# Far scores of a causal attention: two row tiles of 128 columns, or one block-diagonal product of 256

## The chip, the cores and the metric

The kernel runs on one core of one Trainium2 chip. The time is the device time of one execution in microseconds (us), the median over several runs. Before the change it is 4056.7 us over three runs (4050.87 to 4056.8). The profile is of one further execution, which took 4048.82 us, 4047.1 us of them between its first and its last instruction.

## The reference

The block has four batches of 2048 tokens, width 256, 16 heads of 16 dimensions.

```python
q, k, v = split_heads(x @ Wq + bq), split_heads(x @ Wk + bk), split_heads(x @ Wv + bv)
scores = jnp.einsum('bhid,bhjd->bhij', q, k)
rel = jnp.einsum('bhid,pd->bhip', q, rel_key)          # p = 512 relative positions
rel_idx = jnp.clip(j - i + p - 1, 0, p - 1)            # all keys 511 or more back share position 0
bias = jnp.take_along_axis(rel, rel_idx, axis=3)
logits = jnp.where(j <= i, (scores + bias) * scale, -inf)
out = jnp.einsum('bhij,bhjd->bhid', softmax(logits), v) @ Wo + bo
```

The reference calls it as `x + ga * attn(modulated layernorm(x))`, followed by a mixture of eight experts of which each token uses two. Only the attention is touched here.

## The kernel before, in words

The kernel has four phases one after the other: modulation, projection, attention and experts. In the attention, queries and keys are cut into blocks of 128 tokens, 16 blocks a batch. For each row of blocks i the kernel scores key blocks j = 0 to i. A block is **near** if i - j < 5: then each product also needs a bias that depends on the distance. It is **far** otherwise: then all keys share the bias of relative position 0, which is already folded into the keys, and a far score is a plain product.

Queries and keys are float16 pairs of a high and a low part, so that one head's product has a contraction of 3 x 16 rows and one more row that subtracts the row maximum, 49 in all (`KM` = 48). Two heads lie in one tile of 128 partitions: heads 0 to 7 in partitions 0 to 48, heads 8 to 15 in partitions 64 to 112. The keys of both are in `kn[:, j, h]`. The queries are in `qs[:, slot, e, h]`, block-diagonal: `qs` is cleared once and for e = 0 only partitions 0 to 63 are filled, for e = 1 only 64 to 127. A near product (`near_scores`, L775) uses all 113 rows and gets both heads from one weight load, with 32 queries of each. A far product (`far_scores`, L789) names 49 rows of one half, and 128 queries.

Each row of blocks is visited twice. First come its **maxima**, two rows ahead of the scores (`AHEAD` = 2): PE makes the products again in one of three PSUM banks `pm` (`NBUF` = 3), and DVE takes each bank of 512 columns into `acc` by an elementwise maximum (L721 the first, L725 near, L733 far). Then come 16 transposes (`turn`, L816), a reduction over the keys (L736), one more transpose (`rows`, L820), and the maxima go through memory into row 48 of `qs`. The **scores** themselves go to two PSUM tiles `ps` of two banks each. ACT takes the exponential of a tile in one instruction (L758 near, L761 far), and `weigh` (L845) multiplies the values, 32 columns of the array at a time.

The order is written out in `batch`. For each pair (i, j) there are three places: score half 0, score half 1, and weigh the pair before. The list of steps of `max_steps(i + 2)` is spread evenly over the places by its number of entries: a near block gives four steps of one bank, a far block two steps of two banks. Every engine walks the same order. PE may start a maximum only when DVE has emptied the bank it writes to (`mx_done`). Because a far step fills two banks, it waits for the bank two tiles back, `done_count(b, n + 1 - NBUF)`; a near step waits for the one three tiles back.

Of the kernel before, what the change touches and what calls it, by code (L numbers as in the profile page):

```python
# [26 lines left out]
ALU = mybir.AluOpType  # L27
ACT = mybir.ActivationFunctionType
# [7 lines left out]
P = 128  # L36
NB = S // P
EH = E // P
HH = 8
# [4 lines left out]
SCALE = D ** -0.5  # L44
# [420 lines left out]
def phase_attention(nc, io, keep):  # L465
# [4 lines left out]
    AHEAD, SLOTS, NBUF = 2, 4, 3  # L470
    KM = 3 * D
# [12 lines left out]

    def max_steps(i):

        out = []
        for j in key_order(i):
            out += [("near", j, x) for x in range(4)] if near(home(i), j) else [("far", j, r) for r in range(2)]
        return out + [("turn", 0, r) for r in range(4)] + [("rows", 0, 0)]  # L490

    def after_same(i, j):

        js = key_order(i)
        return near(home(i), js[js.index(j) - 1]) == near(home(i), j)

    in_bank = lambda step: 2 if step[0] == "far" else 1
    max_tiles = lambda i: sum(map(in_bank, max_steps(i)))
    first_tile = lambda i: sum(max_tiles(n) for n in range(i))
    NT = first_tile(NB)  # L500
    assert NT % NBUF == 0 and NP % 4 == 0

    def batch_maxima(maximum, b, i, steps, start, stop):
        n = first_tile(i) + sum(map(in_bank, steps[:start]))
        for step in steps[start:stop]:
            maximum(b, i, *step, n)
            n += in_bank(step)

    def batch(b, last, score=None, weigh=None, maximum=None, step=None):

# [32 lines left out]
    with PhaseMemory(nc, "att") as a:  # L543
# [36 lines left out]
        with nc.Block() as block:  # L580
# [126 lines left out]
            @block.vector  # L707
            def _(dve):
                dve.memset(qs[:, :, :, :, :], 0.0).then_inc(cleared, 1)
                dve.memset(tick[:, 0:1], 0.0).then_inc(pair_done[0], HALF)  # L710
                dve.memset(tick[:, 1:2], 0.0).then_inc(pair_done[1], HALF)
                dve.memset(tick[:, 2:3], 0.0).then_inc(mx_done, NBUF)

                def maximum(b, i, kind, j, r, n):
                    u = i % 2
                    if kind == "near":
                        dve.wait_ge(mx_full, b * NT + n + 1)
                        held = acc[:, u, :, r * XQ:(r + 1) * XQ]
                        got = pm[n % NBUF][:, :].rearrange("p (h c) -> p h c", c=XQ)
                        if j == home(i):  # L720
                            dve.tensor_copy(held, got).then_inc(mx_done, 1)  # L721
                        else:

                            dve.wait_ge(mx_done, done_count(b, n - 4 if after_same(i, j) else n - r - 1))
                            dve.tensor_tensor(held, got, held, ALU.max).then_inc(mx_done, 1)  # L725
                    if kind == "far":
                        for e in range(2):
                            dve.wait_ge(mx_full, b * NT + n + e + 1)
                            held = acc[:, u, e * HH + 4 * r:e * HH + 4 * r + 4, :]
                            got = pm[(n + e) % NBUF][:, :].rearrange("p (h c) -> p h c", c=P)  # L730

                            dve.wait_ge(mx_done, done_count(b, n + e - 4 if after_same(i, j) else n - 2 * r - 1))
                            dve.tensor_tensor(held, got, held, ALU.max).then_inc(mx_done, 1)  # L733
                    if kind == "turn":
                        dve.wait_ge(mx_full, b * NT + n + 1)
                        dve.reduce_max(mx[:, u, 4 * r:4 * r + 4], pm[n % NBUF][:, :].rearrange("p (h k) -> p h k", k=P),  # L736
                                       AX.X).then_inc(mx_done, 1)
                    if kind == "rows":
                        dve.wait_ge(mx_full, b * NT + n + 1)
                        dve.wait_ge(m_in[u], b * (NB // 2 * 32) + i // 2 * 32)  # L740
                        dve.tensor_copy(mrow[:, u, :], pm[n % NBUF][0:H, 0:P]).then_inc(mx_done, 1)  # L741

                def weigh(b, i, j, k):
                    if j < i:
                        return
                    dve.wait_ge(pair_done[k % 2], pair_count(b, k))
                    dve.wait_ge(on_out[i % 2], b * (NB // 2 * 16) + i // 2 * 16)
                    dve.tensor_copy(on[:, i % 2], po[:, :, :]).then_inc(on_done, 1)
                order(dve, maximum=maximum, weigh=weigh)

            @block.scalar
            def _(act):
                def score(b, i, j, k, t):
                    act.wait_ge(s_full[t], b * NP + k + 1)

                    act.wait_ge(pair_done[k % 2], pair_count(b, k) - 1)
                    if near(i, j):
                        act.activation(pt[:, k % 2, :, t * 64:t * 64 + 64].rearrange("p h (x c) -> p x h c", x=2),  # L758
                                       ps[t][:, :, :].rearrange("p x (h c) -> p x h c", c=XQ), ACT.Exp, scale=SCALE).then_inc(p_done[t], 1)
                    else:  # L760
                        act.activation(pt[:, k % 2].rearrange("p (e h) c -> p e h c", e=2)[:, :, 4 * t:4 * t + 4, :],  # L761
                                       ps[t][:, :, :].rearrange("p e (h c) -> p e h c", c=P), ACT.Exp, scale=SCALE).then_inc(p_done[t], 1)
                order(act, score=score)

            @block.tensor
            def _(pe):
# [16 lines left out]
                                             start=False, stop=(g == XQ // G - 1), skip_group_check=True)  # L783
                    return last

                def far_scores(bank, i, j, e, h, c):

                    s, rows = i % SLOTS, slice(64 * e, 64 * e + KM + 1)
                    return pe.matmul(bank[:, c * P:(c + 1) * P], kn[rows, j, h, :], qs[rows, s, e, h, :],  # L789
                                     start=True, stop=True, skip_group_check=True)  # L790

                def maximum(b, i, kind, j, r, n):
                    if kind == "near" and j == home(i) and r == 0:
                        pe.wait_ge(qs_in[i % SLOTS], b * (NB // SLOTS * 64) + i // SLOTS * 64 + 64)
                        pe.wait_ge(spread, b * NB + i + 1)
                    if kind == "near":
                        keys = kn[:, j] if i < NB else kx[:, j]
                        if r == 0 and (j == home(i) or i == AHEAD):
                            if i < NB:
                                pe.wait_ge(kv_in[j], b * 80 + 80)  # L800
                            else:
                                pe.wait_ge(kx_in, b * (AHEAD * 64) + AHEAD * 64)
                        pe.wait_ge(mx_done, done_count(b, n - NBUF))
                        near_scores(pm[n % NBUF][:, :], keys, i, j, r, False).then_inc(mx_full, 1)
                    if kind == "far":
                        pe.wait_ge(mx_done, done_count(b, n + 1 - NBUF))
                        pe.wait_ge(built, 80)
                        for c in range(4):
                            for e in range(2):
                                last = far_scores(pm[(n + e) % NBUF][:, :], i, j, e, 4 * r + c, c)  # L810
                                if c == 3:
                                    last.then_inc(mx_full, 1)
                    if kind == "turn":
                        pe.wait_ge(mx_done, done_count(b, max(n - NBUF, n - 1 - r)))
                        for h in range(4):
                            last = pe.transpose(pm[n % NBUF][:, h * P:(h + 1) * P], acc[:, i % 2, 4 * r + h, :], keep["ident"][:, :])  # L816
                        last.then_inc(mx_full, 1)
                    if kind == "rows":
                        pe.wait_ge(mx_done, done_count(b, n - 1))
                        pe.transpose(pm[n % NBUF][0:H, 0:P], mx[:, i % 2, :], keep["ident"][:, :]).then_inc(mx_full, 1)  # L820

                def score(b, i, j, k, t):
# [5 lines left out]
                    if near(i, j):  # L828
                        for x in range(2):
                            last = near_scores(ps[t][:, x], kn[:, j], i, j, 2 * t + x, True)  # L830
                        last.then_inc(s_full[t], 1)
                    else:
                        pe.wait_ge(built, 80)
                        for c in range(4):
                            for e in range(2):
                                last = far_scores(ps[t][:, e], i, j, e, 4 * t + c, c)
                        last.then_inc(s_full[t], 1)

                def weigh(b, i, j, k):
# [704 lines left out]
```

## Time and profile before

| | |
|---|---|
| median of three runs | 4056.7 us |
| profiled execution | 4048.82 us, span 4047.1 us |
| PE busy (matmul) | 3370.2 us, 83% |
| PE weight loads | 2904.3 us, 72% |
| DVE busy | 2355.8 us, 58% |
| ACT busy | 1486.2 us, 37% |
| attention (303.5 to 3053 us) | 2749.5 us |

PE is the matmul engine, DVE the vector engine, ACT the scalar engine and POOL the general one. Matmuls are pipelined: a row "0.40 us, x8" in a timeline is eight matmuls, each of which is shown for some 0.2 us, with much of that lying over its neighbours. So what a group costs PE is the distance from its start to the start of the next group. Ends of matmuls are modelled, and starts are recorded.

### The profile page before, as it was taken

The page shows a single profiled execution, that of the slowest core. Times are in us where ns is not written, and L with a number is a line of the kernel's source. Part 1 is how long each engine was busy: PE and PEld are TensorE (multiplying, and loading weights), DVE is VectorE, ACT ScalarE, POOL GpSimd, SP SyncE. Part 2 cuts the span into 40 slices and gives each one's busy share as a digit, 9 for nine tenths or more (in the row PEclk, how much of TensorE's full clock was granted, in tenths as well). Part 3 has the DMA queues.
Part 4 walks back from the last instruction along what each step waited for, and adds up shares of the span by engine and source line. Part 5 has one row for each costly group of instructions (what it writes and reads, how often), then busy time and mean ns, then how long its engine had stood idle before and what let it go on. Part 6 is the DMA issues. An engine that isn't in the chain of part 4 may idle for free. (4 is left out here: it accounts for less than half of the span.)

```text
span 4047.1 us, 177336 instructions
## 1 busy us (share of the span) xinstructions
PE 3370.2 (83%) x76680; PEld 2904.3 (72%) x76680; DVE 2355.8 (58%) x4401; ACT 1486.2 (37%) x1799; POOL 1093.1 (27%) x936
## 2 busy tenths in 40 slices
PE   6956999999899999999999999999995877599910
PEld 4535887778888777888877788887774766488800
DVE  5844666773566677166667536666722666466633
ACT  1311233446233344623334542334461322255511
POOL 1013311111322111232211133111101555422266
PEclk8977999999999999999999999999996766599955
DMA  4763100001210000310100031000006976333356
GB/s 121 210 154 99 38 24 27 23 23 56 84 31 30 23 23 13 99 46 28 29 21 24 23 106 43 23 23 23 11 9 102 171 141 125 107 116 116 113 166 179
DMA packets 275046, 285.87 MB, mean 71 GB/s; under 512 B 99208, under 2 KB 212716, under 8 KB 274156
## 3 DMA queue, kind: packets, MB, share of 16 engines
q1 hardware_dynamic: 248044, 214.34, 20.5%
q0 software_dynamic: 26240, 60.20, 5.4%
q8 instruction: 621, 10.17, 1.0%
q14 instruction: 141, 1.16, 0.1%
HBM read 165.64 MB, written 107.53 MB: 67 GB/s over the span
## 5 line engine op out<-in xcount | busy, mean ns | idle before, releaser
L758 ACT ACTIVATE att_pt<-att_ps 128x1024 f32<-128x1024 f32 x560 | 574.1, 1025 | 1206.2 <-PE att_ps L782 1206.2
L725 DVE TENSOR_TENSOR att_acc<-att_pm,att_acc 128x512 f32<-128x512 f32 x864 | 570.7, 688 | 351.0 <-PE att_pm L779 343.6
L733 DVE TENSOR_TENSOR att_acc<-att_pm,att_acc 128x512 f32<-128x512 f32 x1056 | 666.3, 685 | 146.2 <-PE att_pm L789 137.7
L779 PE MATMUL att_ps<-att_qx,table_x 68*128 68x64 f16 x8960 | 720.5, 194 | 0.3 <-issue 0.2
L782 PE MATMUL att_ps<-att_qz,table_z 128*128 128x64 f16 x8960 | 717.7, 193 | 0.4 <-issue 0.4
L761 ACT ACTIVATE att_pt<-att_ps 128x1024 f32<-128x1024 f32 x528 | 515.1, 1024 | 381.8 <-PE att_ps L789 380.5
L782 PEld LDWEIGHTS att_ps<-att_qz,table_z 128*128 128x128 f16 x8960 | 613.3, 98 | 0.4 <-issue 0.3
L779 PEld LDWEIGHTS att_ps<-att_qx,table_x 68*128 68x128 f16 x8960 | 610.6, 98 | 1.0 <-issue 1.0
L845 PE MATMUL att_po<-att_pt,att_vn 128*32 128x128 f32 x17408 | 590.1, 276 | 0.5 <-issue 0.3
L683 POOL DMA_DIRECT2D s_m<-att_mrow x64 | 35.3, 552 | 1817.5 <-DVE att_mrow L741 1790.7
L775 PE MATMUL att_pm<-att_qs,att_kn 113*128 113x64 f16 x8672 | 444.7, 195 | 52.0 <-POOL att_qx L668 45.0
L775 PE MATMUL att_ps<-att_qs,att_kn 113*128 113x64 f16 x8960 | 449.1, 193 | 38.7 <-DMA att_qs<-s_m 32.5
L845 PEld LDWEIGHTS att_po<-att_pt,att_vn 128*32 128x32 f32 x17408 | 443.4, 110 | 48.0 <-issue 11.0
L779 PE MATMUL att_pm<-att_qx,table_x 68*128 68x64 f16 x8960 | 455.0, 194 | 1.8 <-issue 1.7
L775 PEld LDWEIGHTS att_pm<-att_qs,att_kn 113*128 113x128 f16 x8672 | 328.8, 99 | 132.3 <-issue 57.1
L775 PEld LDWEIGHTS att_ps<-att_qs,att_kn 113*128 113x128 f16 x8960 | 344.1, 98 | 66.8 <-issue 46.6
L779 PEld LDWEIGHTS att_pm<-att_qx,table_x 68*128 68x128 f16 x8960 | 347.9, 99 | 2.6 <-issue 2.5
L736 DVE TENSOR_REDUCE att_mx<-att_pm 128x4 f32<-128x512 f32 x256 | 172.1, 690 | 282.1 <-PE att_pm L816 282.1
L721 DVE COPY att_acc<-att_pm 128x512 f32<-128x512 f32 x256 | 172.1, 688 | 216.1 <-PE att_pm L779 215.1
L789 PE MATMUL att_pm<-att_qs,att_kn 49*128 49x128 f16 x4224 | 209.5, 219 | 92.5 <-DVE att_acc L733 91.8
L668 POOL TENSOR_TENSOR att_qz<-att_qe,mask_i 128x1024 f16<-128x1024 f16 x128 | 240.4, 1901 | 57.4 <-DMA att_qe<-s_q 56.2
L668 POOL TENSOR_TENSOR att_qx<-att_qe,mask_i 64x1024 f16<-64x1024 f16 x128 | 239.2, 1887 | 0.0
(214 smaller groups left out, 4172.2 us busy)
## 6 DMA issues: line engine op xcount, KB each, us to landing
att_qe<-s_q SPq DMA_DIRECT2D x256, 128.0 KB
moe_xs<-s_h SPq DMA_DIRECT2D x71, 256.0 KB, 2.7
s_y<-moe_y SPq DMA_DIRECT2D x71, 256.0 KB, 2.1
s_v<-prj_vx SPq DMA_DIRECT2D x32, 512.0 KB, 3.7
att_vn<-s_v SPq DMA_DIRECT2D x64, 256.0 KB, 3.4
s_o<-att_on POOLq DMA_DIRECT2D x64, 256.0 KB, 3.2
att_qs<-s_q SPq DMA_DIRECT2D x128, 66.0 KB
prj_x<-in_x POOLq DMA_DIRECT2D x16, 512.0 KB, 4.6
```

Source lines behind the costliest of these rows:

```text
L668: last = pool.tensor_tensor(dst[0:rows, s, :, heads, :], qe[0:rows, i % 2, heads].rearrange("p h (g i) -> p g h i", i=G), keep["mask_i"][0 ...
L721: dve.tensor_copy(held, got).then_inc(mx_done, 1)
L725: dve.tensor_tensor(held, got, held, ALU.max).then_inc(mx_done, 1)
L733: dve.tensor_tensor(held, got, held, ALU.max).then_inc(mx_done, 1)
L736: dve.reduce_max(mx[:, u, 4 * r:4 * r + 4], pm[n % NBUF][:, :].rearrange("p (h k) -> p h k", k=P), AX.X).then_inc(mx_done, 1)
L758: act.activation(pt[:, k % 2, :, t * 64:t * 64 + 64].rearrange("p h (x c) -> p x h c", x=2), ps[t][:, :, :].rearrange("p x (h c) -> p x h ...
L761: act.activation(pt[:, k % 2].rearrange("p (e h) c -> p e h c", e=2)[:, :, 4 * t:4 * t + 4, :], ps[t][:, :, :].rearrange("p e (h c) -> p e ...
L775: pe.matmul(pairs[:, :, h], keys[0:rows, h, :], qs[0:rows, s, :, h, x * XQ:(x + 1) * XQ], start=(h == 0), stop=False, skip_group_check=True)
L779: last = pe.matmul(groups[:, :, g], keep["table_x"][:, y:y + P], qx[0:G * D + G, s, x * (XQ // G) + g], start=False, stop=(g == XQ // G - ...
L782: last = pe.matmul(groups[:, :, g], keep["table_z"][:, y:y + P], qz[:, s, x * (XQ // G) + g], start=False, stop=(g == XQ // G - 1), skip_g ...
L789: return pe.matmul(bank[:, c * P:(c + 1) * P], kn[rows, j, h, :], qs[rows, s, e, h, :], start=True, stop=True, skip_group_check=True)
L845: last = pe.matmul(po[32 * (h % 4):32 * (h % 4) + 32, h // 4, :], vn[:, j, h, :], pt[:, k % 2, h, :], start=(j == 0 and h < 4), stop=(j == ...
```

## The change

A far product now names all 113 rows, as the near one does, and takes the queries of both heads from the block-diagonal `qs`: 2 x 128 = 256 columns from one weight load. One bank of 512 columns is filled by two such products and holds heads h and h + 8 side by side. So a far block of maxima becomes four steps of one bank, in place of two steps of two banks, and waits for the bank three tiles back. The number of banks filled (`NT`), the number of DVE and ACT instructions and their sizes are as they were; their views of `acc` and `pt` follow the new order of heads. Because a far block now has four entries in the list, the even spreading over the places puts the steps of a row elsewhere.

```diff
-            out += [("near", j, x) for x in range(4)] if near(home(i), j) else [("far", j, r) for r in range(2)]
+        out = [("near" if near(home(i), j) else "far", j, x) for j in key_order(i) for x in range(4)]
...
-                    if kind == "far":
-                        for e in range(2):
-                            dve.wait_ge(mx_full, b * NT + n + e + 1)
-                            held = acc[:, u, e * HH + 4 * r:e * HH + 4 * r + 4, :]
-                            got = pm[(n + e) % NBUF][:, :].rearrange("p (h c) -> p h c", c=P)
+                            held = acc[:, u].rearrange("p (e h) c -> p h e c", e=2)[:, 2 * r:2 * r + 2]
+                            got = pm[n % NBUF][:, :].rearrange("p (h e c) -> p h e c", e=2, c=P)
...
-                def far_scores(bank, i, j, e, h, c):
-                    s, rows = i % SLOTS, slice(64 * e, 64 * e + KM + 1)
-                    return pe.matmul(bank[:, c * P:(c + 1) * P], kn[rows, j, h, :], qs[rows, s, e, h, :],
-                                     start=True, stop=True, skip_group_check=True)
+                def far_scores(bank, i, j, r):
+                    s, rows = i % SLOTS, 64 + KM + 1
+                    for h in range(2):
+                        last = pe.matmul(bank[:, 2 * h * P:(2 * h + 2) * P].rearrange("p (e c) -> p e c", c=P), kn[0:rows, j, 2 * r + h, :],
+                                         qs[0:rows, s, :, 2 * r + h, :], start=True, stop=True, skip_group_check=True)
+                    return last
...
                     if kind == "far":
-                        pe.wait_ge(mx_done, done_count(b, n + 1 - NBUF))
-                        pe.wait_ge(built, 80)
-                        for c in range(4):
-                            for e in range(2):
-                                last = far_scores(pm[(n + e) % NBUF][:, :], i, j, e, 4 * r + c, c)
-                                if c == 3:
-                                    last.then_inc(mx_full, 1)
+                        pe.wait_ge(mx_done, done_count(b, n - NBUF))
+                        far_scores(pm[n % NBUF][:, :], i, j, r).then_inc(mx_full, 1)
...
-                        for c in range(4):
-                            for e in range(2):
-                                last = far_scores(ps[t][:, e], i, j, e, 4 * t + c, c)
+                        for x in range(2):
+                            last = far_scores(ps[t][:, x], i, j, 2 * t + x)
```

PE in row 13 of a batch, among its far pairs, before the change. Writes to `att_ps` are scores, to `att_pm` maxima of row 15, to `att_po` the weighing; L775 with L779 is one near maximum.

```order
L845 MATMUL att_po<-att_pt,att_vn 32x128 x16
L806 REGISTER_ALU
L789 MATMUL att_pm<-att_qs,att_kn 128x128 x8
L827 REGISTER_ALU
L789 MATMUL att_ps<-att_qs,att_kn 128x128 x8
L806 REGISTER_ALU
L789 MATMUL att_pm<-att_qs,att_kn 128x128 x8
L789 MATMUL att_ps<-att_qs,att_kn 128x128 x8
L803 REGISTER_ALU
L775 MATMUL att_pm<-att_qs,att_kn 128x2x32 x8
L779 MATMUL att_pm<-att_qx,table_x 128x16x4 x8
L845 MATMUL att_po<-att_pt,att_vn 32x128 x16
```

Here a far maximum fills two banks with eight products, and one stands behind each weighing or score. After the change, in the same row (L766 and L770 are the near maximum, L781 is `far_scores`, L831 the weighing):

```order
L815 REGISTER_ALU
L781 MATMUL att_ps<-att_qs,att_kn 128x256 x4
L799 REGISTER_ALU
L781 MATMUL att_pm<-att_qs,att_kn 128x256 x2
L799 REGISTER_ALU
L781 MATMUL att_pm<-att_qs,att_kn 128x256 x2
L781 MATMUL att_ps<-att_qs,att_kn 128x256 x4
L799 REGISTER_ALU
L781 MATMUL att_pm<-att_qs,att_kn 128x256 x2
L799 REGISTER_ALU
L781 MATMUL att_pm<-att_qs,att_kn 128x256 x2
L831 MATMUL att_po<-att_pt,att_vn 32x128 x16
```

The four banks of a far block now come one by one, two behind each score half, each with a wait of its own.

## Rows read from the trace of the kernel before

**Rows 1.** The page: busy time of each engine, and PE's clock in 40 slices.

```profile
PE 3370.2 (83%) x76680; PEld 2904.3 (72%) x76680; DVE 2355.8 (58%) x4401; ACT 1486.2 (37%) x1799; POOL 1093.1 (27%) x936
PEclk8977999999999999999999999999996766599955
```

**Rows 2.** Windows: length, then busy PE, PEld, DVE, ACT, POOL; clock; DMA.

```profile
303.50:3053.00 2749.50, 2521.25 (x71696) 2222.08 (x71697) 1637.47 (x2559) 1092.47 (x1091) 617.08 (x507) 0.98 0.12 37
1389.50:1443.40 53.90, 49.28 (x1402) 42.55 (x1401) 37.29 (x59) 22.11 (x22) 9.78 (x8) 1.00 0.08 23
1558.60:1618.80 60.20, 55.44 (x1558) 46.82 (x1556) 43.71 (x69) 27.19 (x28) 9.79 (x8) 1.00 0.07 20
3700.00:3712.00 12.00, 11.95 (x107) 10.16 (x105) 8.08 (x15) 7.02 (x13) 3.49 (x3) 1.00 0.39 117
```

**Rows 3.** Groups of instructions on PE, the far products; count, busy, mean ns, idle before.

```profile
L789 PE MATMUL att_pm<-att_qs,att_kn 49*128 49x128 f16 x4224 | 209.5, 219 | 92.5 <-DVE att_acc L733 91.8
L789 PE MATMUL att_ps<-att_qs,att_kn 49*128 49x128 f16 x4224 | 204.6, 218 | 7.6 <-ACT att_pt L761 5.5 <-issue 0.3
```

**Rows 4.** Timeline of PE, row 12 of the second batch: start, length, engine, line.

```profile
1504.23 0.41 PE L775 MATMUL att_pm<-att_qs,att_kn 113*128 113x64 f16 x8
1504.47 0.40 PE L779 MATMUL att_pm<-att_qx,table_x 68*128 68x64 f16 x8
1504.81 0.40 PE L789 MATMUL att_ps<-att_qs,att_kn 49*128 49x128 f16 x8
1505.13 0.41 PE L775 MATMUL att_pm<-att_qs,att_kn 113*128 113x64 f16 x8
1505.38 0.40 PE L779 MATMUL att_pm<-att_qx,table_x 68*128 68x64 f16 x8
1505.71 1.08 PE L845 MATMUL att_po<-att_pt,att_vn 128*32 128x128 f32 x32
1506.72 0.41 PE L775 MATMUL att_pm<-att_qs,att_kn 113*128 113x64 f16 x8
...
1507.30 0.40 PE L789 MATMUL att_ps<-att_qs,att_kn 49*128 49x128 f16 x8
1507.53 0.39 PE L789 MATMUL att_pm<-att_qs,att_kn 49*128 49x128 f16 x8
1507.75 0.39 PE L789 MATMUL att_ps<-att_qs,att_kn 49*128 49x128 f16 x8
1508.87 0.40 PE L789 MATMUL att_pm<-att_qs,att_kn 49*128 49x128 f16 x8 [0.73 <-DVE att_acc L733]
```

**Rows 5.** Timeline of PE in the experts: twelve float16 products of 256 columns.

```profile
3703.16 1.47 PE L1440 MATMUL moe_bank<-moe_h_s,moe_w_s 128*128 128x256 f16 x12
3704.47 1.47 PE L1468 MATMUL moe_bank<-moe_w_s,moe_h_s 128*128 x12
```

**Rows 6.** Waits of PE's matmuls and weight loads: total us, times, longest.

```profile
PE att_pm L789 <- DVE att_acc L733: 91.8, 128, 1.2
PEld att_pm L789 <- DVE att_acc L733: 130.5, 200, 1.3
PEld att_ps L789 <- ACT att_pt L761: 17.7, 57, 0.7
```

**Rows 7.** Groups of instructions on DVE and ACT.

```profile
L733 DVE TENSOR_TENSOR att_acc<-att_pm,att_acc 128x512 f32<-128x512 f32 x1056 | 666.3, 685 | 146.2 <-PE att_pm L789 137.7
L725 DVE TENSOR_TENSOR att_acc<-att_pm,att_acc 128x512 f32<-128x512 f32 x864 | 570.7, 688 | 351.0 <-PE att_pm L779 343.6
L761 ACT ACTIVATE att_pt<-att_ps 128x1024 f32<-128x1024 f32 x528 | 515.1, 1024 | 381.8 <-PE att_ps L789 380.5
```

**Rows 8.** Timeline, fourth batch, row 14: far scores without maxima between.

```profile
2985.16 1.08 PE L845 MATMUL att_po<-att_pt,att_vn 128*32 128x128 f32 x32
2986.18 0.40 PE L789 MATMUL att_ps<-att_qs,att_kn 49*128 49x128 f16 x8
2986.77 0.40 PE L789 MATMUL att_ps<-att_qs,att_kn 49*128 49x128 f16 x8 [0.20 <-ACT att_pt L761]
```

More of the change, by code:

```diff
@@ L485, in max_steps @@
     def max_steps(i):
-        out = []
-        for j in key_order(i):
-            out += [("near", j, x) for x in range(4)] if near(home(i), j) else [("far", j, r) for r in range(2)]
+        out = [("near" if near(home(i), j) else "far", j, x) for j in key_order(i) for x in range(4)]
         return out + [("turn", 0, r) for r in range(4)] + [("rows", 0, 0)]
@@ L495, in after_same @@
         return near(home(i), js[js.index(j) - 1]) == near(home(i), j)
-    in_bank = lambda step: 2 if step[0] == "far" else 1
-    max_tiles = lambda i: sum(map(in_bank, max_steps(i)))
+    max_tiles = lambda i: len(max_steps(i))
     first_tile = lambda i: sum(max_tiles(n) for n in range(i))
@@ L503, in batch_maxima @@
     def batch_maxima(maximum, b, i, steps, start, stop):
-        n = first_tile(i) + sum(map(in_bank, steps[:start]))
-        for step in steps[start:stop]:
+        for n, step in enumerate(steps[start:stop], first_tile(i) + start):
             maximum(b, i, *step, n)
-            n += in_bank(step)
     def batch(b, last, score=None, weigh=None, maximum=None, step=None):
@@ L715, in maximum @@
                     u = i % 2
-                    if kind == "near":
+                    if kind in ("near", "far"):
                         dve.wait_ge(mx_full, b * NT + n + 1)
-                        held = acc[:, u, :, r * XQ:(r + 1) * XQ]
-                        got = pm[n % NBUF][:, :].rearrange("p (h c) -> p h c", c=XQ)
+                        if kind == "near":
+                            held = acc[:, u, :, r * XQ:(r + 1) * XQ]
+                            got = pm[n % NBUF][:, :].rearrange("p (h c) -> p h c", c=XQ)
+                        else:
+                            held = acc[:, u].rearrange("p (e h) c -> p h e c", e=2)[:, 2 * r:2 * r + 2]
+                            got = pm[n % NBUF][:, :].rearrange("p (h e c) -> p h e c", e=2, c=P)
                         if j == home(i):
@@ L724, in maximum @@
                             dve.wait_ge(mx_done, done_count(b, n - 4 if after_same(i, j) else n - r - 1))
-                            dve.tensor_tensor(held, got, held, ALU.max).then_inc(mx_done, 1)
-                    if kind == "far":
-                        for e in range(2):
-                            dve.wait_ge(mx_full, b * NT + n + e + 1)
-                            held = acc[:, u, e * HH + 4 * r:e * HH + 4 * r + 4, :]
-                            got = pm[(n + e) % NBUF][:, :].rearrange("p (h c) -> p h c", c=P)
-                            dve.wait_ge(mx_done, done_count(b, n + e - 4 if after_same(i, j) else n - 2 * r - 1))
                             dve.tensor_tensor(held, got, held, ALU.max).then_inc(mx_done, 1)
@@ L760, in score @@
                     else:
-                        act.activation(pt[:, k % 2].rearrange("p (e h) c -> p e h c", e=2)[:, :, 4 * t:4 * t + 4, :],
-                                       ps[t][:, :, :].rearrange("p e (h c) -> p e h c", c=P), ACT.Exp, scale=SCALE).then_inc(p_done[t], 1)
+                        act.activation(pt[:, k % 2].rearrange("p (e h) c -> p h e c", e=2)[:, 4 * t:4 * t + 4],
+                                       ps[t][:, :, :].rearrange("p x (h e c) -> p (x h) e c", e=2, c=P), ACT.Exp, scale=SCALE).then_inc(p_done[t], 1)
                 order(act, score=score)
@@ L832, in score @@
                     else:
-                        pe.wait_ge(built, 80)
-                        for c in range(4):
-                            for e in range(2):
-                                last = far_scores(ps[t][:, e], i, j, e, 4 * t + c, c)
+                        for x in range(2):
+                            last = far_scores(ps[t][:, x], i, j, 2 * t + x)
                         last.then_inc(s_full[t], 1)
```

## The prediction

> **What bounds the kernel now.** I began with the busy shares [rows 1]: PE leads with 83%, DVE has 58%, ACT 37%. The windows come next, since the change lies in the attention alone. There PE's matmuls fill 2521 of 2749.5 us and DVE is busy for 1637 [rows 2]. In the long rows of blocks it is tighter: row 13 of the second batch lasts 60.2 us, with 55.4 on PE and 43.7 on DVE; row 10 lasts 53.9, with 49.3 and 37.3 [rows 2]. So PE sets the pace and DVE is its nearest rival. The clock is at its upper level, 2.4 GHz, there (1.00). The reader should see two things in PE's rows that a busy share hides: what a far group costs from start to start, and how long PE stands before it.
>
> **The far product in PE's own time.** There are 2 x 4224 far matmuls [rows 3], that is 1056 groups of eight. Where far groups follow one another they start at 1507.30, 1507.53 and 1507.75: 0.23 us for eight products of 128 columns [rows 4]. 1024 columns at 2.4 GHz would be 0.43 us, so the two halves of the array do work side by side. The change gives this up: the same group is four products of 256 columns. The nearest rows are the experts' float16 products of 256 columns, twelve from 3703.16 to 3704.47 at clock 1.00 [rows 2, 5]: 1.31 / 12 = 0.109 us each, 0.436 a group. This adds 0.436 - 0.234 = 0.202 us, times 1056: **+213 us**. (0.234 is the 0.23 of the row, to a digit more than it prints, taken over all such neighbours of the trace.) No row shows this product with two stretches of 128 columns as its moving side. Bounds: 256 columns at 2.4 GHz are 0.107 us, 10 us less in total; the near product with its two stretches of 32 columns takes (1504.47 - 1504.23) / 8 = 0.030 us for 64 columns [rows 4], 0.120 for 256, which would be 46 us more. I take 0.109, the row with the same column count.
>
> **The borders of the far groups.** From L775 to L779 it is 0.24 us, both over the full array. From L779 to a far group it is 0.34 (1504.47 to 1504.81) and from a far group to L775 0.32 (1504.81 to 1505.13), against 0.24 and 0.23 where the kind stays [rows 4]. Each border between a far group and a full-array group so costs 0.096 us, at entry and at exit alike. Counted in the program's order there are 738 unbroken stretches of far groups; 1056 of their ends lie at full-array work and 420 at the weighing L845. The first kind goes: 1056 x 0.096 = **-101 us**. The second stays, as L779 to L845 also takes 0.33 (1505.38 to 1505.71), and L845 to L775 1.01 (1505.71 to 1506.72), where L845 to a far group takes 1.02 (2985.16 to 2986.18) [rows 4, 8]. If the border is not a matter of the row tiles, nothing of the 101 comes back.
>
> The Trainium skill, "TensorEngine Tiling (Array Packing)", has both sides of this. Its section "When to Use Tiling" wants row tiles where the contraction is 64 or less and promises up to twice the speed, which by itself speaks against this change; 49 rows fall under it, and the trace agrees with 0.23 us against 0.43. Its section "Key Properties" says that a change of tiling mode drains the engine, and the borders of 0.096 us agree with that. By the first alone the sum would be 213 us worse before any wait is counted, by both it is 112.
>
> PE's own work therefore grows by 213 - 101 = **112 us**. Fewer weight loads (one for two heads) bring nothing beyond this, since they lie under the products.
>
> **The waits that it can fill.** PE stands before far groups for DVE: 130.5 us by the weight loads, in 200 waits, and for ACT 17.7 us in 57 [rows 6]. By the matmuls it is 91.8 us [rows 6], but their ends are modelled and swallow up to 0.2 us of each wait, so I go by the loads, whose total is 148; some of them hold the ordinary pause behind a weighing, and I take **145** as what can come back. Bounds: 97 (91.8 + 5.5 of [rows 3, 6]) and 148.
>
> Why should it come back? A wait arises because a far step needs two of three banks at once and hands DVE two tiles: DVE needs about 0.63 us for a tile where it runs through (the rows say 685 ns with overlap, 666.3 us for 1056 [rows 7]). At 1508.87 PE stood 0.73 us for this [rows 4]. After the change each tile asks for one bank, the one three tiles back, and DVE's total is untouched. I walk through the piece shown in the order after the change, PE's start at 0 with a near maximum: it ends at 0.48; score half 0.92; first far tile 1.13; second 1.35; score half 1.79; third 2.01; fourth 2.23; weighing to 3.35. DVE, some 0.2 us behind and one tile each 0.63: near tile done 1.33, far tiles 1.97, 2.60, 3.23, 3.87. The third tile starts at 1.79 and needs the near tile's bank (1.33); the fourth starts at 2.01 and needs the first far one's (1.97); the next near tile starts at 3.35 and needs the second's (2.60). Nothing is waited for if DVE starts level, and some 0.1 us if it is a little behind. There are 264 far blocks of maxima, so I leave 20 us of waits between 0 (all gone) and 145 (all kept). The wait for ACT: with no maxima between, a pair of blocks is two exponentials of 0.98 us (515.1 / 528), 1.95 us, while PE has 0.23 + 0.33 + 1.01 = 1.57 us and stands for ACT: its two halves start 0.59 apart, at 2986.18 and 2986.77, in place of 0.23 [rows 7, 8]. After, PE has 0.44 + 0.56 + 1.01 = 2.01, just above. So in those pairs the longer products are mostly under ACT's time already.
>
> The steps of a row move too. In row 13, 44 tiles instead of 40 are now made under its nine far pairs. PE has about 33 us there and DVE 44 x 0.63 = 28, so PE still leads. DVE's and ACT's instructions keep count and size; the new views cost between 681 and 688 ns as all maxima of 512 columns do, under 7 us either way, on an engine with room. SP, POOL and their DMA do not move. The four transposes at the end of a row come in a little denser, with a wait of up to 0.5 us in some of 44 rows, which I cost at 5 us within the 20.
>
> **Sum.** +213 - 101 - 145 + 20 = **-13 us**. Against the profiled execution: 4048.8 - 13 = 4036. That execution lies 8 us below the median of the runs, so against the median it is 4056.7 - 13 = **4043.7 us**. A difference of 0.2% (8 us) is about what a measurement of this kernel tells from none.
>
> **Rivals.**
> - *DVE sets the pace in the far stretches* (slower). The waits stay because they are DVE's work and not its bursts: in row 13 DVE is 73% busy over the whole row, more within a burst of four far tiles, 4 x 0.63 = 2.5 us, for which PE of its own has 4 x 0.109 x 2 + 2 x 0.436 = 1.7 us. If half of the 145 stay the sum is 213 - 101 - 72 = +40, 4097 us; if all stay, +112, 4169 us. It decides as soon as more than 41 us of waits are left. For it: all far waits today name DVE. Against: with a weighing of 1.01 us behind every burst DVE catches up.
> - *No change to be measured.* The gain and the loss are each near 110 us, and 25 to 40 us of remaining waits cancel them: 4049 to 4065 us.
> - *The border cost stays*, as something other than row tiles, for example the change of operands. Then +213 - 145 + 20 = +88, 4145 us. Against: L775 to L779 changes operands as well and shows none [rows 4].
> - *All waits go and the product takes 0.107 us*: 213 - 10 - 101 - 145 = -43, 4014 us.
>
> **How the numbers follow.** My forecast, with the last rival as its lower end, has 0.54 (faster by over 0.2%); no change to be measured 0.22; slower 0.24, of which DVE's pace holds 0.19 and the borders 0.05. The time is the forecast's, 4044. The range begins at 4012, just below the all-gone case of 4014, and goes up to 4080, some 55 us of remaining waits; above lie half of the slower cases. The forecast's own range is 4014 to 4048.
>
> **What would show it.** In the changed profile far groups of four should start 0.44 us apart, the step from L779's line to a far product should be near 0.24 us, and the waits of PE's loads for the far maxima should fall from 130.5 to below 30 us. DVE's busy time should stay within 10 us of 2355.8, and PE's far busy time should rise. I am wrong if the waits stay, if the pitch of the 256-column product is not 0.109, or if waits appear before near maxima or transposes instead.

## The result

Over 20 runs each the changed kernel takes 4043.74 us (4034.22 to 4050.64) and the kernel before 4055.65 us (4038.06 to 4064.22). The ratio is 0.9972, with a 95% interval of 0.9964 to 0.9980: a gain of 0.28%, 11.9 us between the medians. The profiled execution of the changed kernel happens to be its slowest run (4050.64 us, span 4049.0), so spans say little here. What is steady is the attention's own length, and the last start of the weighing marks its end. This is that line for the kernel before and for the changed one (instruction and count; shortest, median and longest ns; first and last start in us):

```profile
L845 PE MATMUL att_po<-att_pt,att_vn x17408: 269/273/422, 378.8 to 3054.5; 128*32 128x128 f32 x198
```

```profile
L831 PE MATMUL att_po<-att_pt,att_vn x17408: 269/273/297, 380.2 to 3046.4; 128*32 128x128 f32 x198
```

The attention ends 8.1 us earlier. I use this mark for all kernels below, and call it the end mark. The first start of the weighing moves between runs too, from 378.8 to 386.3 us, so every difference at the end mark is uncertain by some 5 us, and smaller ones are not read.

### The profile page after: what moved, and what is told of

Its sections match the earlier page's. It is cut to its first block and busy times, and to the rows that moved or that the text cites. A ratio compares the mean times of both kernels' runs of the same rounds, so it can differ in the third digit from the quotient of the medians.

```text
span 4049.0 us, 168239 instructions
## 1 busy us (share of the span) xinstructions
PE 3466.8 (86%) x72456; PEld 3019.6 (75%) x72456; DVE 2363.6 (58%) x4401; ACT 1489.8 (37%) x1799; POOL 1094.9 (27%) x936
## 5 line engine op out<-in xcount | busy, mean ns | idle before, releaser
L770 PE MATMUL att_ps<-att_qx,table_x 68*128 68x64 f16 x8960 | 720.8, 194 | 0.0
L770 PEld LDWEIGHTS att_ps<-att_qx,table_x 68*128 68x128 f16 x8960 | 611.5, 98 | 0.0
L831 PE MATMUL att_po<-att_pt,att_vn 128*32 128x128 f32 x17408 | 588.0, 276 | 0.2 <-ACT att_pt L749 0.2
L831 PEld LDWEIGHTS att_po<-att_pt,att_vn 128*32 128x32 f32 x17408 | 442.1, 109 | 77.4 <-issue 62.4
L766 PE MATMUL att_ps<-att_qs,att_kn 113*128 113x64 f16 x8960 | 447.7, 193 | 41.8 <-DMA att_qs<-s_m 34.5
L766 PE MATMUL att_pm<-att_qs,att_kn 113*128 113x64 f16 x8672 | 440.0, 194 | 47.6 <-POOL att_qx L663 44.8
L770 PE MATMUL att_pm<-att_qx,table_x 68*128 68x64 f16 x8960 | 453.3, 194 | 1.0 <-issue 1.0
L766 PEld LDWEIGHTS att_pm<-att_qs,att_kn 113*128 113x128 f16 x8672 | 347.0, 99 | 95.4 <-issue 59.8
L766 PEld LDWEIGHTS att_ps<-att_qs,att_kn 113*128 113x128 f16 x8960 | 362.7, 98 | 56.4 <-issue 49.4
L781 PE MATMUL att_pm<-att_qs,att_kn 113*128 113x256 f16 x2112 | 355.4, 274 | 1.8
L770 PEld LDWEIGHTS att_pm<-att_qx,table_x 68*128 68x128 f16 x8960 | 346.2, 98 | 1.7 <-issue 1.6
L781 PE MATMUL att_ps<-att_qs,att_kn 113*128 113x256 f16 x2112 | 310.2, 273 | 0.9
```

The lines of the kernel that those rows point to most:

```text
L766: pe.matmul(pairs[:, :, h], keys[0:rows, h, :], qs[0:rows, s, :, h, x * XQ:(x + 1) * XQ], start=(h == 0), stop=False, skip_group_check=True)
L770: last = pe.matmul(groups[:, :, g], keep["table_x"][:, y:y + P], qx[0:G * D + G, s, x * (XQ // G) + g], start=False, stop=(g == XQ // G - ...
L781: last = pe.matmul(bank[:, 2 * h * P:(2 * h + 2) * P].rearrange("p (e c) -> p e c", c=P), kn[0:rows, j, 2 * r + h, :], qs[0:rows, s, :, 2 ...
L831: last = pe.matmul(po[32 * (h % 4):32 * (h % 4) + 32, h // 4, :], vn[:, j, h, :], pt[:, k % 2, h, :], start=(j == 0 and h < 4), stop=(j == ...
```

## The profile after

The page's first row and the window of the attention (columns as in [rows 1, 2]):

```profile
PE 3466.8 (86%) x72456; PEld 3019.6 (75%) x72456; DVE 2363.6 (58%) x4401; ACT 1489.8 (37%) x1799; POOL 1094.9 (27%) x936
...
L781 PE MATMUL att_pm<-att_qs,att_kn 113*128 113x256 f16 x2112 | 355.4, 274 | 1.8
```

```profile
303.50:3053.00 2749.50, 2613.04 (x67512) 2332.20 (x67509) 1641.43 (x2560) 1097.12 (x1091) 616.91 (x508) 0.98 0.12 37
```

PE is busy for 92 us more in the same window as in [rows 2], and has 4224 products fewer. DVE is within 4 us of its old time there. The stretch that answers to [rows 4], in the timeline of PE:

```profile
1505.06 0.40 PE L766 MATMUL att_pm<-att_qs,att_kn 113*128 113x64 f16 x8
1505.29 0.40 PE L770 MATMUL att_pm<-att_qx,table_x 68*128 68x64 f16 x8
1505.53 0.60 PE L781 MATMUL att_ps<-att_qs,att_kn 113*128 113x256 f16 x4
1505.97 0.40 PE L766 MATMUL att_pm<-att_qs,att_kn 113*128 113x64 f16 x8
...
1507.76 0.61 PE L781 MATMUL att_pm<-att_qs,att_kn 113*128 113x256 f16 x4
1508.21 0.60 PE L781 MATMUL att_ps<-att_qs,att_kn 113*128 113x256 f16 x4
1508.65 0.38 PE L781 MATMUL att_pm<-att_qs,att_kn 113*128 113x256 f16 x2
```

Four products of 256 columns take 0.44 to 0.45 us (1505.53 to 1505.97, 1507.76 to 1508.21 and 1508.21 to 1508.65). From the near group L770 to the far group it is now 0.24, where [rows 4] have 0.34: the border is gone. The old far group between two full-array groups took 0.32 from its own start, and 0.42 with its entry; the new one takes 0.44. Waits of PE's weight loads:

```profile
PEld att_pm L808 <- DVE att_mx L727: 64.1, 58, 1.4
...
PEld att_pm L804 <- DVE att_acc L724: 38.5, 37, 1.3
PEld att_pm L781 <- DVE att_acc L724: 30.3, 136, 0.4
PEld att_pm L766 <- DVE att_acc L724: 22.3, 95, 0.5
...
PEld att_ps L781 <- ACT att_pt L752: 7.7, 28, 0.4
```

Far maxima now wait 30.3 us in 136 pauses of 0.22 us, about the ordinary pause behind a weighing, where [rows 6] had 130.5 us in 200. This fall of 100 us overstates what was won, since another 100 pauses of 0.2 us before far maxima are now listed without a releaser:

```profile
PEld att_pm L781 <- issue: 19.8, 100, 0.2
```

By the matmuls, 91.8 us of waits for DVE became none: the row of far maxima in the page above has 1.8 us idle in all. The loads' waits behind ACT fell from 17.7 to 7.7 us.

## The experiments

Each was timed beside the kernel before, and the ratio is to that. The table comes first; "end" is the end mark, "far waits" the row of PE's loads for far maxima behind DVE, as above. Under "products" stands how far products are made, under "places" how the steps of a row are spread: "old" as in the kernel before, "new" as in the changed one.

| kernel | products | banks a step | places | ratio (95%) | end, us | far waits, us |
|---|---|---|---|---|---|---|
| before | half array | 2 | old | 1 | 3054.5 | 130.5 |
| e6 | half array | 2 | new | 0.9920 (0.9906 to 0.9933) | 3021.2 | 85.9 |
| e1 | full, 256 columns | 2 | old | 1.0105 (1.0090 to 1.0121) | 3095.4 | 89.9 |
| e5 | full, 256 columns | 1 | old | 1.0061 (1.0048 to 1.0075) | 3077.6 | 71.4 |
| after | full, 256 columns | 1 | new | 0.9972 (0.9964 to 0.9980) | 3046.4 | 30.3 |
| e7 | full, 128 columns | 1 | new | 0.9994 (0.9984 to 1.0005) | 3051.5 | 18.3 |
| e2 | half array, by banks | 1 | new | 0.9956 (0.9942 to 0.9970) | 3035.8 | 54.8 |
| e3 | scores full, maxima half | 2 | old | 1.0056 (1.0043 to 1.0070) | 3075.3 | 116.9 |
| e4 | maxima full, scores half | 1 | new | 0.9944 (0.9930 to 0.9957) | 3027.0 | 30.0 |
| e8 | mixed by place | both | own | 0.9760 (0.9745 to 0.9775) | 2961.0 | 25.1 + 8.7 |
| e9 | e8, last transpose late | both | own | 0.9733 (0.9711 to 0.9755) | 2941.8 | 25.1 + 11.9 |
| e10 | after, last transpose late | 1 | new, but for it | 0.9824 (0.9806 to 0.9842) | 2984.6 | 33.3 |
| e11 | e9, turns apart | both | own | 0.9630 (0.9608 to 0.9652) | 2907.3 | 25.1 + 6.3 |

Where two far waits stand, the first is of half-array and the second of full-array maxima.

**e1: the new products in the old steps.** `max_steps` and the places are those of before; a far step fills two banks with two calls of the new `far_scores`.

```diff
                     if kind == "far":
                         pe.wait_ge(mx_done, done_count(b, n + 1 - NBUF))
+                        for e in range(2):
+                            far_scores(pm[(n + e) % NBUF][:, :], i, j, 2 * r + e).then_inc(mx_full, 1)
```

> The products of the changed kernel (113 rows, 256 columns) in the steps of the kernel before: a far block of maxima is two steps of two banks, each waits for the bank two tiles back, and the places are the old ones. Theory A (the waits went because each tile asks for one bank): PE keeps at least half of its 145 us of waits before far groups, so the attention is 2741 + 50 to 120 us long, 1.2% to 3% above the changed kernel. Rival B (the waits went because PE itself became longer there and DVE caught up): under 30 us of waits beyond those of the changed kernel, attention 2741 to 2770 us, ratio to the kernel before 0.995 to 1.005.

It ends 49.0 us behind the changed kernel and 40.9 behind the one before. The 49.0 are just under theory A's 50 to 120 us, the ratios are 1.3% apart, inside A's 1.2% to 3%, and 89.9 us of far waits are left; all is far from B's values. But A is not shown by it alone, since two things differ from the changed kernel: banks a step, and places. Its far waits:

```profile
PEld att_pm L790 <- DVE att_acc L733: 89.9, 130, 1.2
```

**e5: the changed kernel with the old places.**

```diff
-                upto = total * (place + 1) // places
+                old = [n for n, s in enumerate(steps) if s[0] != "far" or s[2] % 2 == 0] + [total]
+                upto = old[(len(old) - 1) * (place + 1) // places]
```

> The changed kernel, one bank a step with its own wait, but the steps are put at the places of the kernel before (two one-bank steps where one two-bank step stood). Theory: the spreading matters little, attention 2741 to 2755 us, ratio to before 0.997 to 1.000. Rival (the finer spreading over the places is what filled the waits): 30 to 80 us more than the changed kernel.

The rival holds: 31.2 us more than the changed kernel, from the places alone. Its far waits are 71.4 us in 168 waits of up to 1.0 us:

```profile
PEld att_pm L782 <- DVE att_acc L725: 71.4, 168, 1.0
```

So of the 49.0 us between e1 and the changed kernel 17.8 belong to one bank a step and 31.2 to the places, each uncertain by some 5 us (by the ratios it is about 18 and 36).

**e6: the kernel before with the new places.**

```diff
+                ends = [sum(map(in_bank, steps[:n + 1])) for n in range(total)]
+                tiles = sum(map(in_bank, steps))
-                upto = total * (place + 1) // places
+                upto = sum(e <= tiles * (place + 1) // places for e in ends)
```

> The kernel before, with half-array products and two-bank steps, but its steps are spread by banks and not by entries of the list, so that a row's maxima stand where the changed kernel has them. 992 borders in place of 1056, so 6 us less for these. Theory (spreading alone does little): waits within 30 us of the 145 of before, attention 2725 to 2775, ratio 0.994 to 1.007. Rival (spreading is what removes the waits): below 2650, ratio under 0.98.

It gains 33.3 us at the end mark, 0.8% in time, of which 992 borders in place of 1056 make 6. I had allowed at most 0.6%, and the rival wanted 2% or more: neither held. This small edit alone beats the whole change. What it does can be read in the order of the program. The list gives a far step the same share of places as a near one, though it brings DVE two tiles, so here and there two far steps, four tiles, fall into one place. Counted over the rows of one batch, 17 places of the kernel before hold four tiles of maxima, and 2 places of e6; e5 has 17 and the changed kernel 2. Here is DVE with the far maxima of PE in such a place, late in row 9 of the second batch:

```profile
1371.11 0.40 PE L789 MATMUL att_pm<-att_qs,att_kn 49*128 49x128 f16 x8
1371.54 2.48 DVE L733 TENSOR_TENSOR att_acc<-att_pm,att_acc 128x512 f32<-128x512 f32 x4
1372.29 0.40 PE L789 MATMUL att_pm<-att_qs,att_kn 49*128 49x128 f16 x8 [0.78 <-DVE att_acc L733]
1374.21 0.40 PE L789 MATMUL att_pm<-att_qs,att_kn 49*128 49x128 f16 x8
1374.64 1.29 DVE L733 TENSOR_TENSOR att_acc<-att_pm,att_acc 128x512 f32<-128x512 f32 x2 [0.61 <-PE att_pm L789]
...
1376.56 2.63 DVE L733 TENSOR_TENSOR att_acc<-att_pm,att_acc 128x512 f32<-128x512 f32 x4 [0.63 <-PE att_pm L789]
...
1379.25 0.66 PE L816 MATMUL att_pm<-ident,att_acc 128*128 128x128 f32 x4 [1.38 <-DVE att_acc L733]
```

Two far steps in one place (1371.11 and 1372.29) hand DVE four tiles, 2.48 us of work, and PE stands 0.78 us; behind the next single step DVE stands 0.61 us for PE. Even spreading makes such places rare, but it does not take all waits away: e6 still has 85.9 us of far waits in 161, 44.6 less than before, and its waits before the turns rose by 11.4 us (from 20.7 and 16.4 to 31.1 and 17.4).

```profile
PEld att_pm L791 <- DVE att_acc L735: 85.9, 161, 1.2
```

That the 33.3 us come from the places is shown. That they come from the places of four tiles above all is argued from this count and this stretch; the even spreading moves other steps as well.

**e2: one bank a step from one half of the array.** Four products of 49 rows fill a bank, for scores too.

```diff
-                    s, rows = i % SLOTS, 64 + KM + 1
-                    for h in range(2):
...
+                    s, e = i % SLOTS, r % 2
+                    rows = slice(64 * e, 64 * e + KM + 1)
+                    for c in range(4):
+                        last = pe.matmul(bank[:, c * P:(c + 1) * P], kn[rows, j, 4 * (r // 2) + c, :], qs[rows, s, e, 4 * (r // 2) + c, :],
+                                         start=True, stop=True, skip_group_check=True)
```

> The steps, banks and order of the changed kernel, but each bank of a far block is filled by four products of 49 rows and 128 columns of one half of the array, one after the other, so PE streams the same 512 columns a bank and the two kinds of array use alternate again. In the program's order 1136 borders between half-array and full-array groups stand, where the changed kernel has none. Theory (a border costs 0.096 us because the array's division changes): attention 2741 + 109 = 2850 us, about 4150 in all, ratio to before 1.024 (1.018 to 1.030). Rival (the border belongs to something else of the old far groups, for example two banks written at once): no more than 20 us above the changed kernel, ratio 0.997 to 1.002.

Neither held: it is faster than the changed kernel. My premise was wrong, that four products of one half followed by four of the other run one after the other. The timeline of PE shows otherwise:

```profile
1506.63 0.40 PE L766 MATMUL att_pm<-att_qs,att_kn 113*128 113x64 f16 x8
1506.87 0.40 PE L770 MATMUL att_pm<-att_qx,table_x 68*128 68x64 f16 x8
1507.20 0.41 PE L782 MATMUL att_ps<-att_qs,att_kn 49*128 49x128 f16 x8
1507.44 0.38 PE L782 MATMUL att_pm<-att_qs,att_kn 49*128 49x128 f16 x4
1507.66 0.40 PE L782 MATMUL att_ps<-att_qs,att_kn 49*128 49x128 f16 x8
```

A score half of eight, four of one half of the array and then four of the other, still takes 0.24 us (1507.44 is the next start), while the bank of four after it, alone in its half, takes 0.22. And the border stands: L770 to the far group is 0.33 us, 0.24 in the changed kernel. So the border belongs to half-array products as such and not to two banks written at once, which is what the run was to tell, if not in the way expected. How much of e2's lead over the changed kernel (10.6 us) comes from scores and how much from maxima that overlap was not taken apart.

**e7: 128 columns over the full array.**

```diff
                     for h in range(2):
-                        last = pe.matmul(bank[:, 2 * h * P:(2 * h + 2) * P].rearrange("p (e c) -> p e c", c=P), kn[0:rows, j, 2 * r + h, :],
-                                         qs[0:rows, s, :, 2 * r + h, :], start=True, stop=True, skip_group_check=True)
+                        for e in range(2):
+                            last = pe.matmul(bank[:, (2 * h + e) * P:(2 * h + e + 1) * P], kn[0:rows, j, 2 * r + h, :],
+                                             qs[0:rows, s, e, 2 * r + h, :], start=True, stop=True, skip_group_check=True)
```

> The changed kernel with each product of 256 columns as two of 128 columns over the full 113 rows, with one weight load each: the same columns, twice the products and weight loads, no border. Theory (PE pays by columns, weight loads lie under them): 0.055 us a product, 8448 in all, attention 2741 + 5 to 20 us, ratio to before 0.998 to 1.003. Rival (the weight loads saved are part of the gain): 0.065 us or more a product, +85 us, ratio 1.018 or more.

As the theory has it. Twice the weight loads and products cost 5 us at the end mark and 9 by the ratios. PE pays by columns:

```profile
1506.83 0.62 PE L782 MATMUL att_pm<-att_qs,att_kn 113*128 113x128 f16 x8
1507.29 0.61 PE L782 MATMUL att_ps<-att_qs,att_kn 113*128 113x128 f16 x8
1507.73 0.39 PE L782 MATMUL att_pm<-att_qs,att_kn 113*128 113x128 f16 x4
```

Eight products of 128 columns take 0.44 to 0.46 us, as four of 256 do.

**e3 and e4: one half of the change each.** e3 takes the new product for the scores only; e4 takes it for the maxima only, with their one-bank steps and the new places.

> Only the far scores as 256-column products of the full array; far maxima as before, half-array, two banks a step. 656 borders are left of 1056. Sum: 2749 + 528 x 0.202 = +107, - 400 x 0.096 = -38, less the waits that the longer scores fill. Theory (the one-bank step is what removes the waits): waits before far maxima keep at least 90 us, attention 2775 to 2815 us, ratio to before 1.007 to 1.016. Rival (longer products fill the waits anyway): 2730 to 2765, ratio 0.995 to 1.004.

> Only the far maxima changed: full array, 256 columns, one bank a step; far scores half-array as before. 784 borders are left. Sum against the changed kernel: 2741 - 528 x 0.202 + 784 x 0.096 = 2741 - 107 + 75 = 2709 us of attention, plus what DVE or ACT then hold back (5 to 30 us): 2714 to 2740, ratio to before 0.987 to 0.997. Rival (borders cost nothing when the second kind is a full-array far group): 2634 to 2665, ratio 0.97 to 0.98.

e3 loses 20.8 us at the end mark (it kept 116.9 us of far waits, as expected, but its ratio of 1.0056 is a little better than the range). e4 gains 27.5 and lies inside its range. Together they make -6.7, and the whole change makes -8.1: the two halves add. But e4 has the new places, which in the old products were worth 33.3 us by themselves (e6). Beside e6, which has these places too, e4 ends 5.8 us later and the changed kernel 25.2 us later (3021.2 against 3027.0 and 3046.4): with the places evened out neither half of the change gains, and the scores are the half that hurts.

**e8: each product where it is cheap.** A half-array group of eight costs 0.234 us plus 0.096 for each border to full-array work. Between two full-array groups this is 0.426, no better than 0.436 of the full array. Among far groups and weighings it is 0.234. So far scores are half-array again; far maxima are so only behind a far score; all others are full-array; near maxima among far scores stand only behind a weighing, but for the first pair of a row. The order is a list for each row; `first`, the empty list and `third` are what stands behind score half 0, behind score half 1 and behind the weighing of a pair:

```python
        for j in range(max(0, row - NJ + 1)):
            first, third = [], []
            if j == 0:
                first, closes = closes[:2], closes[2:]
            elif halves:
                first = [("far2",) + halves.pop(0)]
            third, closes = closes[:2], closes[2:]
            parts += [first, [], third]
```

> A mixture: far scores as half-array products again; of the far maxima those made among the far scores also as half-array products in two-bank steps (one a pair, behind score half 0), the others, among the near scores, as full-array one-bank steps. Near maxima among far scores stand only behind a weighing, two a pair. 672 groups of eight half-array products are left, with 283 borders. By the terms found: 2741 - 672 x 0.202 + 283 x 0.096 = 2632 us of attention if no wait comes back; with 10 to 40 us of waits for DVE 2640 to 2675, ratio to before about 0.975 (0.970 to 0.983). Rival (DVE sets the pace once PE has less to do): waits of over 80 us for DVE and a ratio of 0.99 or more.

The ratio is 0.976 and the end 2961.0, 85.4 us before the changed kernel. The terms 672 x 0.202 - 283 x 0.096 gave 109 without waits. The waits behind ACT grew from 7.7 to 25.6 us, where scores stand without maxima, which is most of the rest.

**e9, e10, e11: the end of a row.** In all kernels so far PE stands 58 times for 1.1 to 1.2 us before the last transpose of a row, 64.1 us in the changed kernel (the L808 row above) and 63.4 before the change. e10 is the changed kernel with that step alone in the last place; e9 is the same in the hybrid; e11 is e9 with the four turns apart from the last maxima as well.

```diff
-                upto = total * (place + 1) // places
+                upto = total if place + 1 == places else (total - 1) * (place + 1) // (places - 1)
```

> The changed kernel with the same move: the last transpose alone in a row's last place, all other steps spread over the places before it. PE's loads stand 58 times and 64.1 us for DVE's last reduction there. Theory: 45 to 60 us less than the changed kernel, ratio to before 0.983 to 0.987. Rival (the waits move to the turns or the far maxima, since the rest is denser): less than 20 us gained, 0.993 or more.

> The hybrid (0.976 of before, attention 2659 us), and besides the last transpose of a row (the step called rows, for which PE waits until DVE has reduced the fourth turn) alone in the last place, behind the weighing; the turns stand one place earlier. In the hybrid PE's loads stand for this 58 times, 69.9 us in all. Theory (the weighing of 1.01 us covers the reduction): 45 to 60 us less, ratio to before 0.961 to 0.966. Rival (the wait only moves to the turns, which need the last maxima of the row): within 15 us of the hybrid, 0.973 or more.

> The hybrid with all four turns apart from the last maxima: two behind each of the last two score halves of a row, the last transpose alone behind the weighing, and the maxima spread over the places before. In the version with only the last transpose moved the turns waited 55.9 us for the last maxima in 53 waits of 1.05 us. Theory (a score half of 1.4 us between the last maximum and the first turn covers it): 25 to 45 us less, ratio to before 0.962 to 0.967. Rival (the maxima, now in fewer places, wait instead): within 10 us of that version, 0.971 or more.

e10 reached 0.9824 (0.9806 to 0.9842), a little more than expected; its end, 2984.6, is 61.8 us before the changed kernel's. The wait before the last transpose fell from 64.1 to 25.4 us and the one before the turns from 38.5 to 21.4, 55.8 us together. e9 reached only 0.9733 (0.9711 to 0.9755), in the rival's range, though its end is 19.2 us before e8's where the rival allowed 15. Its last transposes wait less and its first turns more, since they now stood in one place with the row's last maximum. e9's rows:

```profile
PEld att_pm L875 <- DVE att_acc L775: 55.9, 53, 1.3
...
PEld att_pm L879 <- DVE att_mx L785: 30.2, 64, 1.4
```

e11 moved the turns too and reached 0.9630 (0.9608 to 0.9652), 3897.33 us against 4051.11 us beside it, inside its range. The attention ends at 2907.3, 147 us before the kernel before. Of the 55.9 us before the turns 11.8 are left, and 21.6 of the 30.2 before the last transpose:

```profile
PEld att_ps L847 <- ACT att_pt L811: 25.5, 72, 0.7
PEld att_pm L847 <- DVE att_acc L776: 25.1, 112, 0.2
PEld att_pm L880 <- DVE att_mx L786: 21.6, 64, 1.2
...
PEld att_pm L876 <- DVE att_acc L776: 11.8, 37, 1.3
```

## Why the prediction was right, and where not

The forecast was 4044 us and -13 us of change; measured are 4043.74 us, -11.9 us between the medians and -8.1 us at the end mark. The cost terms were right. The term of the waits came out right for a reason that was mostly not the one given, and in that the forecast was lucky.

- **The product, +213 us.** It measured 0.44 us a group against 0.436. Right; e7 shows that it is columns and not weight loads.
- **The borders, -101 us.** The step into a far group fell from 0.34 to 0.24 us at every place looked at; e2 keeps half-array products and keeps the border. Right, and the rival of a border that stays is out.
- **The waits, -145 + 20.** The attention ended 8.1 us earlier, while PE's own work grew by 112 us by the two terms above, so 120 us of waits went, against the 125 forecast. The sum is right. The reason given for it is right in a small part only. I wrote that they go because "each tile asks for one bank". The runs split the 120: 71 had already gone in e1, where steps and places were old and PE was merely slower (112 less 40.9); one bank a step gave 17.8 (e1 to e5); the places gave 31.2 (e5 to after).
- **"The steps of a row move too".** I costed this at nothing beside a denser end of the row. It was worth 31.2 us in the new products and 33.3 in the old ones (e6), more than the whole change. This is the step of the prediction that failed. I had counted how many tiles a stretch holds, 44 for 40, and not how many fall into one place.
- **DVE's pace as a rival.** It did not decide, yet its threshold was near: with the old places the change loses (e5, 1.0061). Had the list not changed its number of entries, the forecast would have had the wrong sign.
- **The places at the row's end** were costed within the 20. The wait before the turns (L804) rose from 37.1 us (20.7 and 16.4) to 38.5, nothing to speak of. But e10 gains 62 us at that end, and the wait it goes for was as long in the kernel before (63.4 us, L820). The prediction does not mention it.
- **Smaller slips.** After the change, two score halves and a weighing add up to 0.44 + 0.54 + 1.01 = 1.99 us, not 2.01; that is still just above ACT's 1.95, so nothing hangs on it. And the promise of up to twice the speed, which the prediction takes from the Trainium skill, "TensorEngine Tiling (Array Packing)", stands in the section "Theoretical Speedup" there, not in "When to Use Tiling".

The 71 us that e1 fills can be checked against the waits of PE's loads for DVE and ACT in the attention. They add up to 318 us in the kernel before and 252 in e1, 66 less: 41 before far maxima, 13 before near maxima, 9 before far scores (behind ACT) and 3 before the turns. So most of it lies where the prediction looked, but the longer products filled it and not the one-bank step. Some 17 us of this fall are ordinary pauses of 0.2 us that e1 lists without a releaser (13.9 us of them before far maxima), so 50 to 66 of the 71 us are found as waits. The rest stays open.

## What to carry to other kernels

A product over half the array is worth it only beside its like: count the borders before comparing columns. When a list is spread evenly over places, spread it by the work of the engine that consumes it, not by its entries; here that edit alone (33.3 us, e6) was worth more than the change that brought it along by accident (8.1 us). And a total that comes out right can rest on a wrong reason: undo each accompanying edit alone.

## What the runs showed of the hardware

- A border between half-array and full-array products costs 0.096 us in each direction (0.34 and 0.33 us from start to start in place of 0.24, in the kernel before and in e2), so eight half-array products of 128 columns between two full-array groups (0.426 us) cost what four full-array products of 256 columns do (0.436 us).
- Products of the two halves of the array run side by side even when four of one half are issued before four of the other: 0.24 us for the eight in e2, against 0.23 when they alternate (before).
- Doubling the weight loads and products at equal columns (e7) cost 5 to 9 us over 4224 additional loads, 1 to 2 ns each.
